# One queue or two for the loads of the first attention in a four-layer cross-attention kernel

## Chip, core and metric

The kernel runs on one core of one Trainium2 chip. The metric is the device time of one execution in microseconds (us), the median of several runs.

## What is computed

Sixteen sequences of 56 tokens with 256 channels (`x`) pass through four layers. Each of them attends to the same memory, `ctx`: 1500 keys with 128 channels for every sequence. The change concerns the first layer alone, which has a single head:

```python
memory_proj    = einsum('bme,de->bmd', memory, W_mem)              # memory: 16 x 1500 x 128
scores         = einsum('bnd,bmd->bnm', hidden_states, memory_proj) / sqrt(D)
attn           = softmax(scores, axis=-1)
memory_context = einsum('bnm,bmd->bnd', attn, memory_proj)
gate           = sigmoid(concat([hidden_states, memory_context]) @ W_gate + b_gate)
x              = rmsnorm(hidden_states + gate * memory_context)
```

Layers 2 and 4 are attention with 16 heads and a feed-forward part, layer 3 is self-attention, narrow cross-attention and a gated MLP. They take most of the time, and nothing in them is changed.

## The kernel before

**Products are reassociated.** `W_mem` is applied to the 56 queries (`pe_q0`), so the 1500 keys are used as they come from memory. That takes every batch of `ctx` in two layouts: *in channels* (`kt0`, from the input `ctxT`, 128 channels x 1500 keys, 750 KB), which the scores need, and *in keys* (`kn0`, from `ctx`, 125 partitions x 12 keys x 128 channels, 672 + 78 KB in two transfers), which the weighted sums need. Both lie in the big tile `q_and_o`, in four buffers each, one per batch: batch b is in buffer b % 4.

**Units.** Two batches make a unit u, so there are 8 units (`L0U`), and the four buffers of a layout hold two units. `pe_l0` runs ten steps s on TensorE (PE). Step s has, in this order: the scores of unit s (L639, 6 matmuls, which the trace counts as 12), the weighted sums of unit s-2 (L651, 24 matmuls, in the trace 48), and the transposes of the probabilities of unit s-1 (L665, 12). In step 0 and 1 there are no sums, in steps 8 and 9 no scores. The end of the scores of a third of the keys counts up `s_sc` (in the listings `s_scores`), so `s_sc` is 3(u+1) when the scores of unit u are complete. The end of the sums of unit u brings `s_pv` (in the listings `s_sums`) to u+1. VectorE (DVE) takes the maxima (L700) and normalises (L717); ScalarE (ACT) exponentiates (L684); both copy the transposed probabilities out of PSUM (L675, ACT two thirds, DVE one third).

**Who loads.** The channels are loaded by SyncE (SP) in `sp_l0_keysT`: batches 0 to 3 at once, and from batch 4 on unit u when the scores of unit u-2 are done (`on.wait_ge(s_sc, 3 * (u - 1))`), since these used the same buffers. The keys are loaded by ACT in `act_l0_keys`: units 0 and 1 at the start of `act_l0`, which is after the barrier that ends the query products, then unit s in step s, between the exponential of unit s and the copies of unit s-1, when the sums of unit s-2 are done (`on.wait_ge(s_pv, u - 1)`). SP and ACT each have a hardware queue of their own (q1 and q10 in the profile). A wait holds only the instruction stream of the engine that waits.

**After the last load.** SP issues the loads of the gate stage (`sp_l0_gate`, L729 to L735: `W_memT`, `W_gateT`, `b_gate`, `norm_w`, `x`, some 1.8 MB), on which `pe_l0_gate` waits, then waits at the barrier that ends the first attention, and issues the loads of the second layer (`sp_gated_a`, L817 on). The gate stage starts at L741 behind that barrier.

Of the kernel before, what the change touches and what calls it, by code (L numbers as in the profile page):

```python
# [14 lines left out]
B, S, D, C, KEYS = 16, 56, 256, 128, 1500  # L15
# [7 lines left out]
KP, KT = 125, 12  # L23
# [15 lines left out]
L0U = B // 2  # L39
# [59 lines left out]
def build(nc, io, out):  # L99
    with ExitStack() as ctx:  # L100
        def sem(name):
            return ctx.enter_context(nc.semaphore(name))
# [118 lines left out]
        kt0 = [QO_flat[:, i * KEYS:(i + 1) * KEYS] for i in range(4)]  # L221
        kn0 = [QO_flat[:, 4 * KEYS + i * KT * C:4 * KEYS + (i + 1) * KT * C] for i in range(4)]
# [58 lines left out]
        s_l0_kt = [sem(f"s_l0_keysT{i}") for i in range(4)]  # L281
        s_l0_kn = [sem(f"s_l0_keys{i}") for i in range(4)]
# [6 lines left out]
        s_sc, s_mx, s_nx = sem("s_scores"), sem("s_max"), sem("s_negmax")  # L289
        s_ex, s_rc = sem("s_exp"), sem("s_recip")  # L290
        s_tr, s_eh, s_el = sem("s_transposed"), sem("s_high"), sem("s_low")
        s_pv, s_ov = sem("s_sums"), sem("s_o_out")
# [22 lines left out]
        def join(e, on, n):  # L315

            e.drain().then_inc(s_join, 1)
            on.wait_ge(s_join, ENGINES * n)
# [296 lines left out]

        ctx_rows = io["ctx"].rearrange("b (p k) c -> b p (k c)", p=KP)

        def sp_l0_keysT(e, on):
            for b in range(B):
                if b >= 4:  # L620
                    on.wait_ge(s_sc, 3 * ((b - 4) // 2 + 1))
                e.dma_start(kt0[b % 4], io["ctxT"][b]).then_inc(s_l0_kt[b % 4], 16)

        def act_l0_keys(e, on, u):
            for b in (2 * u, 2 * u + 1):
                if u >= 2:
                    on.wait_ge(s_pv, u - 1)
                for lo, hi in ((0, 112), (112, KP)):
                    e.dma_start(kn0[b % 4][lo:hi, :], ctx_rows[b, lo:hi, :]).then_inc(s_l0_kn[b % 4], 16)

        def pe_l0(e, on):
            for s in range(L0U + 2):
# [37 lines left out]
        def l0_evacuate(e, on, u, c, done):  # L670
            on.wait_ge(s_tr, 3 * u + c + 1)
            on.wait_ge(s_pv, u - 1)
            dst = l0_p_T[u % 2][0:KP, 4 * c:4 * c + 4, 0:128]
            src = psum[3 + c][0:KP, :].rearrange("p (k r) -> p k r", k=4)
            x = e.copy(dst, src) if c < 2 else e.tensor_copy(dst, src)  # L675
            x.then_inc(done, 1)

        def act_l0(e, on):
            act_l0_keys(e, on, 0)
            act_l0_keys(e, on, 1)  # L680
            for s in range(L0U + 1):
                if s < L0U:
                    on.wait_ge(s_nx, s + 1)
                    e.activation(l0_scores[s % 2], l0_scores[s % 2], ACT.Exp, bias=mx[:, s % 2, 3:4],  # L684
                                 accum_out=mx[:, s % 2, 4:5]).then_inc(s_ex, 1)
                if 2 <= s < L0U:
                    act_l0_keys(e, on, s)
                if s:
                    for c in range(2):
                        l0_evacuate(e, on, s - 1, c, s_l0_ea)  # L690
            join(e, on, J["l0"])
# [35 lines left out]
        def sp_l0_gate(e, on):  # L727
            w = s_w["l0b"]
            e.dma_start(w_memT, io["W_memT"]).then_inc(w, 16)  # L729
            e.dma_start(w_gateT, io["W_gateT"].rearrange("(k p) n -> p k n", p=128)).then_inc(w, 16)  # L730
            e.dma_start(b_gate, io["b_gate"].to_broadcast([128, D])).then_inc(w, 16)
            e.dma_start(norm_w, io["norm_w"].to_broadcast([128, D])).then_inc(w, 16)
            e.dma_start(X, io["x"]).then_inc(w, 16)
            e.dma_start(vecs, io["vectors"]).then_inc(s_const, 16)
            e.dma_start(gates, io["gates"].to_broadcast([128, 4])).then_inc(s_const, 16)  # L735
# [79 lines left out]
        def sp_gated_a(e, on, l):  # L815
            w = s_w[f"l{l}a"]
            e.dma_start(g_wq, io[f"L{l}_Wq"].rearrange("(k p) n -> p k n", p=128)).then_inc(s_w[f"l{l}q"], 16)  # L817
            e.dma_start(g_wkT, io[f"L{l}_WkT"].rearrange("(k p) n -> p k n", p=128)).then_inc(w, 16)
            e.dma_start(value_w, io[f"L{l}_Wkv"][:, INNER:2 * INNER]).then_inc(w, 16)

        def sp_gated_b(e, on, l):
            e.dma_start(g_w1, io[f"L{l}_W1"].rearrange("(k p) n -> p k n", p=128)).then_inc(s_w[f"l{l}u"], 16)
            e.dma_start(g_w2.rearrange("p (k n) -> p k n", k=8), io[f"L{l}_W2"].rearrange("(k p) n -> p k n", p=128)).then_inc(s_w[f"l{l}d"], 16)
# [145 lines left out]
        def sp_wo(e, on, x, l):  # L969

            on.wait_ge(*x.scores((B - 1) * RT - 1, 2))
            on.wait_ge(*x.sums((B - 1) * NG - 1))
            wo = io[f"L{l}_Wo"].rearrange("(k p) n -> p k n", p=128)
            e.dma_start(wo_a.rearrange("p (k n) -> p k n", k=6), wo[:, 0:6, :]).then_inc(s_w[f"l{l}o"], 16)
            e.dma_start(wo_b.rearrange("p (k n) -> p k n", k=2), wo[:, 6:8, :]).then_inc(s_w[f"l{l}o"], 16)

        def sp_cross(e, on, x, first):
            def keysT(b):
                if b >= 2:
                    on.wait_ge(*x.scores((b - 1) * RT - 1, 2))  # L980
                e.dma_start(kt_raw[b % 2], io["ctxT"][b]).then_inc(s_ktl[b % 2], 16)

            def keys(b):
                if b >= 2:
                    on.wait_ge(*x.sums((b - 1) * NG - 1))
                for lo, hi in ((0, 112), (112, KP)):
                    e.dma_start(kn_raw[b % 2][lo:hi, :], ctx_rows[b, lo:hi, :]).then_inc(s_knl[b % 2], 16)

            def mask(b):
                if b:  # L990
                    on.wait_ge(*x.mask(b - 1))
                e.dma_start(mask_raw, io["mask"][b:b + 1, :].to_broadcast([128, KEYS])).then_inc(s_ml, 16)

            if first:
                keysT(0), keys(0), mask(0)
                keysT(1), keys(1)
            else:
                mask(1)
                for b in range(2, B):
                    mask(b), keysT(b), keys(b)  # L1000
# [359 lines left out]
        def sp_l2a(e, on):  # L1360
            on.wait_ge(*prod.made[g1.down[NT - 1]])
            w = s_w["l2a"]
            e.dma_start(wcq, io["L2_cq_w"].rearrange("(k p) n -> p k n", p=128)).then_inc(w, 16)
            e.dma_start(value_w[:, 0:2 * C], io["L2_ckv_w"]).then_inc(w, 16)
            e.dma_start(wcd, io["L2_cdense_w"]).then_inc(w, 16)
# [355 lines left out]
        def sp_narrow(e, on):  # L1721
            for b in range(B):
                if b == 1:
                    on.wait_ge(s_join, ENGINES * J["l2q"])
                if b >= 2:
                    on.wait_ge(s_n_prod, 6 * (b - 1))
                e.dma_start(KT2[b % 2], io["ctxT"][b]).then_inc(s_n_ctx[b % 2], 16)
# [320 lines left out]
        def sync(e):  # L2048
            on = Passed(e)
            w = s_w["l0"]  # L2050
            e.dma_start(w_mem, io["W_mem"].rearrange("(k p) c -> p k c", p=128)).then_inc(w, 16)
            e.dma_start(XT[:, 0:2, :], io["xT"]).then_inc(w, 16)
            e.dma_start(ident, io["ident"]).then_inc(w, 16)
            sp_l0_keysT(e, on)
            sp_l0_gate(e, on)
            on.wait_ge(s_join, ENGINES * J["l0"])
            sp_gated_a(e, on, 1)
            sp_cross(e, on, layers[0], True)
            on.wait_ge(s_join, ENGINES * J["l1q"])
            sp_cross(e, on, layers[0], False)  # L2060
            sp_wo(e, on, layers[0], 1)
            on.wait_ge(s_join, ENGINES * J["l1"])
            sp_gated_b(e, on, 1)
            sp_experts(e, on)
            sp_l2a(e, on)
            sp_narrow(e, on)
            sp_l2b(e, on)
            sp_cross(e, on, layers[1], True)
            on.wait_ge(*prod.made[gu_prod["up", 1, len(IT) - 1, 1]])
            sp_gated_a(e, on, 3)  # L2070
            sp_cross(e, on, layers[1], False)
            sp_wo(e, on, layers[1], 3)
            on.wait_ge(s_join, ENGINES * J["l3"])
            sp_gated_b(e, on, 3)
            on.wait_ge(s_join, ENGINES * J["l3ff"])
            e.dma_start(out, X).then_inc(s_out, 16)
            on.wait_ge(s_out, 16)
# [151 lines left out]
```

## Times and profile before

| | us |
|---|---|
| median of 3 runs | 2423.84 (2419.64 to 2424.02) |
| the profiled execution | 2411.01 |
| its span in the trace | 2409.2 |
| first attention in it, up to the gate stage's first matmul | 114.18 |

| engine | busy in the span |
|---|---|
| PE | 2312.6 us (96%) |
| DVE | 1577.1 us (65%) |
| ACT | 1279.2 us (53%) |
| POOL | 629.1 us (26%) |

The profile is of one execution. Shares over the whole span are means over layers with different limits. The first attention is under 5% of the span, so it has to be read by itself, in the stretch from 0 to 114 us.

### The profile page before, as it was taken

The page shows a single profiled execution, that of the slowest core. Times are in us where ns is not written, and L with a number is a line of the kernel's source. Part 1 is how long each engine was busy: PE and PEld are TensorE (multiplying, and loading weights), DVE is VectorE, ACT ScalarE, POOL GpSimd, SP SyncE. Part 2 cuts the span into 40 slices and gives each one's busy share as a digit, 9 for nine tenths or more (in the row PEclk, how much of TensorE's full clock was granted, in tenths as well). Part 3 has the DMA queues.
Part 4 walks back from the last instruction along what each step waited for, and adds up shares of the span by engine and source line. Part 5 has one row for each costly group of instructions (what it writes and reads, how often), then busy time and mean ns, then how long its engine had stood idle before and what let it go on. Part 6 is the DMA issues. An engine that isn't in the chain of part 4 may idle for free.

```text
span 2409.2 us, 41153 instructions
## 1 busy us (share of the span) xinstructions
PE 2312.6 (96%) x16032; PEld 1883.6 (78%) x16032; DVE 1577.1 (65%) x4254; ACT 1279.2 (53%) x2184; POOL 629.1 (26%) x692
## 2 busy tenths in 40 slices
PE   7978999999999999799999999899999999999999
PEld 3857999999999895456666666456799999999988
DVE  3357777777777657577777776313777777777764
ACT  1235555555555533277777777212555555555553
POOL 0024344443433315200000000010444444343330
PEclk8989999999999999899999999899999999999999
DMA  8810111121110110010000000310011212111010
GB/s 266 221 62 20 46 42 52 37 58 35 54 45 27 54 36 21 14 39 27 27 27 27 27 14 1 125 35 1 20 47 41 59 30 59 42 46 46 27 53 16
DMA packets 36131, 115.96 MB, mean 48 GB/s; under 512 B 4618, under 2 KB 18546, under 8 KB 35938
## 3 DMA queue, kind: packets, MB, share of 16 engines
q1 hardware_dynamic: 33474, 101.04, 13.8%
q10 hardware_dynamic: 2464, 12.29, 2.0%
q8 instruction: 128, 2.10, 0.4%
q14 instruction: 65, 0.53, 0.1%
HBM read 112.40 MB, written 0.92 MB: 47 GB/s over the span
## 4 chain that ended last, share of the span: by engine, by line
PE 89%; ACT 5%; DVE 4%; DMA 1%; issue 0%; ACTq 0%; SPq 0%; DVEq 0%
PE bank L1026 20%; PE bank L1013 19%; PE bank L1038 12%; PE bank L1773 7%; PE bank L555 7%; PE bank L1760 3%; PE bank L1998 3%; PE bank L1786 3%; ACT n_scores L1860 3%; PE bank L651 2%; PE bank L2010 2%; PE bank L1742 2%; PE bank L848 1%; PE bank L1746 1%; PE bank L1224 1%; PE bank L1048 1%
## 5 line engine op out<-in xcount | busy, mean ns | idle before, releaser
L1087 ACT CAST p_T_high<-bank 125x512 fp32r<-125x512 f32 x672 | 350.8, 595 | 516.8 <-PE bank L1038 516.8
L1160 DVE TENSOR_TENSOR p_T_low<-bank,p_T_high 125x512 fp32r<-125x512 f32 x672 | 422.6, 684 | 256.7 <-ACT p_T_high L1087 256.5
L1126 DVE CUSTOM_DVE_ANT_0 scores<-bank,mask 128x500 f32<-128x500 f32 x672 | 418.3, 672 | 1.6 <-PE bank L1013 1.6
L1097 ACT ACTIVATE scores<-scores,row_max 128x1500 f32<-128x1500 f32 x224 | 353.4, 1578 | 9.8 <-DVE row_max L1131 9.8
L1026 PE MATMUL bank<-p_T_high,keys_nat_high 125*128 125x256 f32 (+1 forms) x1152 | 346.0, 300 | 1.7 <-ACT inverse L1094 1.7
L1026 PE MATMUL bank<-p_T_high,keys_nat_low 125*128 125x256 f32 (+1 forms) x1152 | 346.3, 301 | 0.0
L1026 PE MATMUL bank<-p_T_low,keys_nat_high 125*128 125x256 f32 (+1 forms) x1152 | 346.2, 300 | 0.0
L1038 PE MATMUL bank<-ident,scores 128*125 128x128 f32 x2688 | 331.7, 273 | 1.5 <-ACT scores L1097 1.5
L1038 PEld LDWEIGHTS bank<-ident,scores 128*125 128x125 f32 x2688 | 319.0, 188 | 4.2 <-ACT scores L1097 4.1
L1893 DVE CUSTOM_DVE_ANT_0 n_scores<-bank,n_zeros 112x500 f32<-112x500 f32 x384 | 237.4, 674 | 91.9 <-PE bank L1760 91.9
L1013 PE MATMUL bank<-keys_T_high,q_stage_high 128*128 128x500 f32 x672 | 282.0, 420 | 11.8 <-DVE q_stage_low L1103 6.9
L1773 PEld LDWEIGHTS bank<-ident,n_scores 112*125 112x125 f32 x1536 | 187.2, 191 | 115.5 <-issue 54.9
L1013 PE MATMUL bank<-keys_T_high,q_stage_low 128*128 128x500 f32 x672 | 262.6, 391 | 0.0
L1013 PE MATMUL bank<-keys_T_low,q_stage_high 128*128 128x500 f32 x672 | 262.1, 390 | 0.0
L1773 PE MATMUL bank<-ident,n_scores 112*125 112x112 f32 x1536 | 218.3, 286 | 10.3 <-ACT q_and_o L1852 5.8
L1026 PEld LDWEIGHTS bank<-p_T_high,keys_nat_high 125*128 125x128 f32 x1152 | 216.7, 188 | 10.2 <-ACT inverse L1094 2.2
L1026 PEld LDWEIGHTS bank<-p_T_low,keys_nat_high 125*128 125x128 f32 x1152 | 217.0, 188 | 8.5
L1026 PEld LDWEIGHTS bank<-p_T_high,keys_nat_low 125*128 125x128 f32 x1152 | 216.7, 188 | 0.0
L1860 ACT ACTIVATE n_scores<-n_scores,n_stats 112x1500 f32<-112x1500 f32 x128 | 197.7, 1546 | 0.4 <-DVE n_stats L1899 0.4
L1166 POOL CAST q_stage_high<-q_and_o 128x256 fp32r<-128x256 f32 (+1 forms) x94 | 41.5, 441 | 427.6 <-PE bank L1013 427.5
L1013 PEld LDWEIGHTS bank<-keys_T_high,q_stage_high 128*128 128x128 f32 x672 | 127.7, 190 | 32.2 <-issue 8.3
L1013 PEld LDWEIGHTS bank<-keys_T_high,q_stage_low 128*128 128x128 f32 x672 | 127.1, 189 | 26.6
(237 smaller groups left out, 3492.6 us busy)
## 6 DMA issues: line engine op xcount, KB each, us to landing
ctx_T<-in_ctxT SPq DMA_DIRECT2D x32, 750.0 KB, 4.2
ctx_nat<-in_ctx SPq DMA_DIRECT2D x32, 672.0 KB
q_and_o<-in_ctxT SPq DMA_DIRECT2D x16, 750.0 KB, 9.7
n_ctx_T<-in_ctxT SPq DMA_DIRECT2D x16, 750.0 KB, 4.2
q_and_o<-in_ctx ACTq DMA_DIRECT2D x16, 672.0 KB
mask_bytes<-in_mask SPq DMA_DIRECT2D x32, 187.5 KB, 5.2
weights<-in_L_W SPq DMA_DIRECT2D x4, 1024.0 KB, 6.2
ctx_nat<-in_ctx SPq DMA_DIRECT2D x32, 78.0 KB
```

The source lines that it names most:

```text
L555: x = e.matmul(out, left[i], right[j], start=start and n == 0, stop=stop and n == 2)
L1013: m = e.matmul(psum[c][:, 0:CHK], QSs[i][g % 2][:, lo:lo + 128], KTs[j][b % 2][:, cols], start=(n == 0), stop=(n == 2))
L1026: m = e.matmul(psum[6 + g % 2][:, cols_g], KNs[i][b % 2][0:KP, cols], PTs[j][g % 2][0:KP, k, cols_g], start=(k == 0 and n == 0), stop=(k = ...
L1038: m = e.transpose(psum[3 + c][0:KP, 128 * k:128 * k + 128], SB[u % 2][:, (4 * c + k) * KP:(4 * c + k + 1) * KP], ident)
L1087: e.copy(PTs[0][g % 2][0:KP, 4 * c:4 * c + 4, lo:lo + 128], psum[3 + c][0:KP, :].rearrange("p (k r) -> p k r", k=4)).then_inc(s_eh, 1)
L1097: e.activation(SB[s % 2], SB[s % 2], ACT.Exp, bias=mx[:, s % 4, 3:4], accum_out=mx[:, s % 4, 4:5]).then_inc(s_ex, 1)
L1126: e.tensor_tensor_reduce(out=SB[u % 2][:, c * CHK:(c + 1) * CHK], in0=psum[c][:, 0:CHK], in1=mb[:, c * CHK:(c + 1) * CHK], scale=1.0, scal ...
L1160: e.tensor_tensor(low, psum[3 + c][0:KP, :].rearrange("p (k r) -> p k r", k=4), high.bitcast(F32), ALU.subtract).then_inc(s_el, 1)
L1760: e.matmul(psum[r][0:PAIR, 0:CHK], n_q[b % 2][rows, PAIR * hh:PAIR * hh + PAIR], CK[b % 2][rows, c * CHK:(c + 1) * CHK], start=True, stop= ...
L1773: m = e.transpose(psum[4 + t % 2][0:KP, PAIR * k:PAIR * k + PAIR], n_unit(quad, r)[0:PAIR, at:at + KP], ident[0:PAIR, 0:PAIR])
L1860: e.activation(unit, unit, ACT.Exp, bias=n_st[0:PAIR, quad % 2, r, 3:4], accum_out=n_st[0:PAIR, quad % 2, r, 4:5]).then_inc(s_n_ex, 1)
L1893: e.tensor_tensor_reduce(out=n_unit(quad, r)[0:PAIR, c * CHK:(c + 1) * CHK], in0=psum[r][0:PAIR, 0:CHK], in1=n_zeros[0:PAIR, :], scale=1.0 ...
```

## The change

All loads of the memory for the first attention are issued by SP, in one instruction stream and one queue. `act_l0_keys` is gone from ACT. The order in SP's stream is: channels of units 0 and 1, keys of units 0 and 1, then for u = 2 to 7 the channels of unit u and the keys of unit u, each with the wait it had before. The loads of the gate stage follow behind the keys of unit 7.

```diff
-        def sp_l0_keysT(e, on):
-            for b in range(B):
-                if b >= 4:
-                    on.wait_ge(s_sc, 3 * ((b - 4) // 2 + 1))
-                e.dma_start(kt0[b % 4], io["ctxT"][b]).then_inc(s_l0_kt[b % 4], 16)
-
-        def act_l0_keys(e, on, u):
-            for b in (2 * u, 2 * u + 1):
-                if u >= 2:
-                    on.wait_ge(s_pv, u - 1)
-                for lo, hi in ((0, 112), (112, KP)):
-                    e.dma_start(kn0[b % 4][lo:hi, :], ctx_rows[b, lo:hi, :]).then_inc(s_l0_kn[b % 4], 16)
+        def sp_l0_keys(e, on):
+            def in_channels(u):
+                for b in (2 * u, 2 * u + 1):
+                    if u >= 2:
+                        on.wait_ge(s_sc, 3 * (u - 1))
+                    e.dma_start(kt0[b % 4], io["ctxT"][b]).then_inc(s_l0_kt[b % 4], 16)
+
+            def in_keys(u):
+                for b in (2 * u, 2 * u + 1):
+                    if u >= 2:
+                        on.wait_ge(s_pv, u - 1)
+                    for lo, hi in ((0, 112), (112, KP)):
+                        e.dma_start(kn0[b % 4][lo:hi, :], ctx_rows[b, lo:hi, :]).then_inc(s_l0_kn[b % 4], 16)
+
+            in_channels(0), in_channels(1)
+            in_keys(0), in_keys(1)
+            for u in range(2, L0U):
+                in_channels(u)
+                in_keys(u)
...
         def act_l0(e, on):
-            act_l0_keys(e, on, 0)
-            act_l0_keys(e, on, 1)
             for s in range(L0U + 1):
                 if s < L0U:
                     on.wait_ge(s_nx, s + 1)
                     e.activation(l0_scores[s % 2], l0_scores[s % 2], ACT.Exp, bias=mx[:, s % 2, 3:4],
                                  accum_out=mx[:, s % 2, 4:5]).then_inc(s_ex, 1)
-                if 2 <= s < L0U:
-                    act_l0_keys(e, on, s)
                 if s:
                     for c in range(2):
                         l0_evacuate(e, on, s - 1, c, s_l0_ea)
...
-            sp_l0_keysT(e, on)
+            sp_l0_keys(e, on)
```

SP's stream in the first attention before. After the four channels without a wait come those of units 2 and 3 (the pattern goes on to unit 7), in pairs:

```order
L622 DMA q_and_o<-in_ctxT 128x1500 x4
L622 DMA q_and_o<-in_ctxT 128x1500 [waits s_scores]
L622 DMA q_and_o<-in_ctxT 128x1500
L622 DMA q_and_o<-in_ctxT 128x1500 [waits s_scores]
L622 DMA q_and_o<-in_ctxT 128x1500
```

The same stream now, from the channels of unit 2 to those of unit 3:

```order
L623 DMA q_and_o<-in_ctxT 128x1500 [waits s_scores]
L623 DMA q_and_o<-in_ctxT 128x1500
L630 DMA q_and_o<-in_ctx 112x1536 [waits s_sums]
L630 DMA q_and_o<-in_ctx 13x1536
L630 DMA q_and_o<-in_ctx 112x1536
L630 DMA q_and_o<-in_ctx 13x1536
L623 DMA q_and_o<-in_ctxT 128x1500 [waits s_scores]
L623 DMA q_and_o<-in_ctxT 128x1500
```

Between the two pairs of channels there are now four transfers of keys, the first of which waits for `s_sums`, that is, for the weighted sums of unit 0.

PE's stream in step 3 is the same before and now. The scores of unit 3 (first and second row: the channels of its two batches), the sums of unit 1, and the start of the transposes of unit 2:

```order
L639 MATMUL bank0<-q_and_o 64x500 [waits s_max,s_l0_keysT2]
L639 MATMUL bank0<-q_and_o 64x500 [waits s_l0_keysT3]
L639 MATMUL bank1<-q_and_o 64x500 [waits s_max]
L639 MATMUL bank1<-q_and_o 64x500
L639 MATMUL bank2<-q_and_o 64x500 [waits s_max]
L639 MATMUL bank2<-q_and_o 64x500
L651 MATMUL bank7<-area,q_and_o 128x64 [waits s_l0_keys2,s_l0_evac_dve,s_l0_evac_act]
L651 MATMUL bank7<-area,q_and_o 128x64 x11
L651 MATMUL bank7<-area,q_and_o 128x64 [waits s_l0_keys3]
L651 MATMUL bank7<-area,q_and_o 128x64 x11
L665 MATMUL bank3<-ident,area 125x128 [waits s_l0_normed]
```

Nothing moved here: the sums of a unit stand behind the scores of the unit that comes two later.

ACT's stream before, from the exponential of unit 2 to that of unit 3:

```order
L684 ACTIVATE area,row_max<-area,row_max 128x1500 [waits s_negmax]
L629 DMA q_and_o<-in_ctx 112x1536 [waits s_sums]
L629 DMA q_and_o<-in_ctx 13x1536
L629 DMA q_and_o<-in_ctx 112x1536
L629 DMA q_and_o<-in_ctx 13x1536
L675 COPY area<-bank3 125x4x128 [waits s_transposed]
L675 COPY area<-bank4 125x4x128 [waits s_transposed]
```

and now, where the copies follow the exponential directly (the rows of units 2 and 3):

```order
L689 ACTIVATE area,row_max<-area,row_max 128x1500 [waits s_negmax]
L682 COPY area<-bank3 125x4x128 [waits s_transposed]
L682 COPY area<-bank4 125x4x128 [waits s_transposed]
L689 ACTIVATE area,row_max<-area,row_max 128x1500 [waits s_negmax]
L682 COPY area<-bank3 125x4x128 [waits s_sums,s_transposed]
```

## Rows read from the trace of the kernel before

**Rows 1.** The page: busy time of each engine, then the chain by engine.
```profile
PE 2312.6 (96%) x16032; PEld 1883.6 (78%) x16032; DVE 1577.1 (65%) x4254; ACT 1279.2 (53%) x2184; POOL 629.1 (26%) x692
...
PE 89%; ACT 5%; DVE 4%; DMA 1%; issue 0%; ACTq 0%; SPq 0%; DVEq 0%
```

**Rows 2.** Chain that ended last, first attention: start us, us, what.
```profile
14.76 4.32 PE bank L639 x12
19.46 14.90 DMA q_and_o<-in_ctxT
34.41 5.26 PE bank L639 x10
39.67 5.52 PE bank L651 x48
45.19 1.36 PE bank L665 x12
46.55 2.67 PE bank L639 x12
49.22 5.50 PE bank L651 x48
...
87.34 5.52 PE bank L651 x48
94.28 0.42 ACTq L629
94.75 1.08 ACT area L675 x2
95.87 8.86 PE bank L651 x48
104.73 2.66 PE bank L665 x12
...
114.18 3.29 PE bank L741 x14
```

**Rows 3.** Waits: line waited for: us in total, times, longest us.
```profile
PE bank L639 <- DMA q_and_o<-in_ctxT: 8.0, 2, 6.0
PE bank L651 <- ACT area L675: 1.7, 1, 1.7
...
SPq L622 <- PE bank L639: 59.5, 6, 17.1
```

**Rows 4.** Timeline: start us, us, engine, line, count, in brackets the idle before.
```profile
2.20 66.93 SPq L622 DMA_DIRECT2D q_and_o<-in_ctxT  x16
14.78 3.99 ACTq L629 DMA_DIRECT2D q_and_o<-in_ctx  x8
30.49 1.93 PE L639 MATMUL bank<-q_and_o 128*64 128x500 f32 x2 [5.99 <-DMA q_and_o<-in_ctxT]
94.25 0.69 DVE L675 COPY area<-bank 125x512 f32<-125x512 f32 x1
```

**Rows 5.** Stretches: from:to, busy us, last the granted clock, DMA share, GB/s.
```profile
2.00:13.90 11.90, 6.10 (x8) 2.52 (x8) 0.62 (x1) 1.07 (x1) 0.97 (x1) 1.00 0.96 349
19.10:34.40 15.30, 6.11 (x26) 2.25 (x22) 5.71 (x15) 4.23 (x6) 0.00 (x0) 0.83 1.01 273
34.41:39.67 5.26, 5.26 (x11) 1.30 (x11) 1.37 (x4) 0.00 (x0) 0.00 (x0) 0.50 0.49 202
39.67:45.20 5.53, 5.53 (x50) 5.53 (x51) 0.84 (x3) 1.64 (x2) 0.00 (x0) 1.00 0.78 280
94.20:97.90 3.70, 2.04 (x18) 2.03 (x18) 0.74 (x2) 1.07 (x2) 0.00 (x0) 0.97 1.04 237
98.00:107.40 9.40, 9.39 (x44) 9.10 (x43) 0.28 (x1) 1.17 (x2) 0.00 (x0) 0.50 0.49 126
116.00:124.00 8.00, 7.28 (x28) 4.99 (x27) 2.33 (x6) 3.79 (x6) 4.51 (x4) 1.00 1.04 383
124.00:128.00 4.00, 4.00 (x21) 3.51 (x20) 0.66 (x2) 0.50 (x2) 3.92 (x4) 1.00 1.03 263
```

## Prediction

> **What bounds the kernel now.** I read the page first. PE is busy for 96% of the span and makes up 89% of the chain [rows 1]. That is a mean over four layers, and the change touches only the first 114 us, so the next view is the chain of waits there [rows 2]. The reader is to see two regimes. Once it runs, the chain is PE alone: sums 5.50 us, transposes 1.36, scores 2.67, and again. From 49.22 to 87.34 us that is four steps, 9.53 us each. Loads don't show in it, because the channels of unit u+1 are asked for a whole step before PE wants them. At 19.46 the chain shows the other regime: 14.90 us of a transfer in channels, then ten score matmuls in 5.26 us. There PE outran the loads.
>
> The waits say the same [rows 3]. PE waited for channels twice, 8.0 us in total, and for a copy by ACT once, 1.7 us. SP spent 59.5 us in six waits for the scores: it is early, and sits ready when a buffer comes free. That readiness is what the change touches.
>
> The last view is the stretches with clock and bandwidth [rows 5]. The ten score matmuls after the wait ran at a granted clock of 0.50, that is 1.2 of 2.4 GHz, 0.53 us each against 2.67/12 = 0.22 us at 1.00. PE had idled 5.99 us before the first pair of them [rows 4]. So a wait of PE for a load costs the wait and a slow start.
>
> **The change, part by part.** Let T(s) be the end of the sums in step s. Before, T(2) is 45.19 and T(7) is 87.34 + 5.52 = 92.86 [rows 2].
>
> *The wait in front of the channels.* SP now meets the keys of unit u, which wait for `s_pv` = u-1, before it may issue the channels of unit u+1. That count comes at T(u), from the sums in step u. PE wants the channels of unit u+1 as soon as it has done the transposes, 1.36 us after T(u). Before, they were issued at the end of the scores in step u-1, a step and a half earlier. Now six issues stand between T(u) and the scores, and the keys lie ahead of the channels in the same queue: two keys, then two channels, 4 x 768 KB = 3.07 MB. This comes five times, for the scores of units 3 to 7.
>
> How long? For the channels the nearest row is the pair issued at 39.67: in 5.53 us 280 GB/s moved 1.55 MB, which is the pair (1.536 MB), with the DMA engines busy for 0.78 of it, 4.3 us. So 1.2 us pass before data flow, and the pair takes 4.3 [rows 5]. For the keys the row nearest to one layout alone is 124 to 128 us, the second layer's keys and mask from SP's queue, at 263 GB/s: 1.536/0.263 = 5.8 us. Sum 1.2 + 5.8 + 4.3 = 11.3 us from T(u) to the second batch of channels. Bounds: all at the best stretch, 383 GB/s, 1.2 + 8.0 = 9.2 us; all at the worst full one, 237 GB/s, 1.2 + 13.0 = 14.2 us [rows 5].
>
> The 16 DMA engines top out at 435 GB/s by the Trainium skill (DMA: Bandwidth & Descriptors, Specifications); by that figure, as an estimate, the two pairs take 8.3 us with the start, and the sum below comes out 15 us lower. No stretch here reaches it: the best is 383 [rows 5].
>
> *The slow start.* When the second batch lands, one score matmul pair is done and ten remain, as at 34.41: 5.26 us at half clock. The idle before the first batch is longer here (about 7.7 us) than the 5.99 there [rows 4]. The sums behind them then run at full clock, 5.52, as from 39.67 [rows 5]. Step: 11.3 + 5.3 + 5.5 = 22.1 us instead of 9.53. Five steps: 110.5 instead of 47.7 us.
>
> *The start.* The first keys are issued behind the first channels at about 4 us, not at 14.78 after the barrier [rows 4]. They can't move sooner than the channels are through, at about 13.9 (from 2 to then 349 GB/s moved the 4.2 MB issued first) [rows 5]. Keys of four batches and channels of unit 2 are 4.6 MB; at the 273 GB/s that this mix had from 19.1 to 34.4 [rows 5] they land by 13.9 + 16.9 = 30.8 instead of 34.4. T(2) becomes 30.8 + 5.3 + 5.5 = 41.6, a gain of 3.6 us. Then T(7) = 41.6 + 110.5 = 152.1 instead of 92.86.
>
> *ACT without the issues.* In steps 3 to 7 ACT's four issues (1.6 us) lay beside the sums and scores, so taking them out is worth nothing there. At the end they show: ACT copied at 94.75 behind its last issue, at 94.28, and PE waited until 95.87 [rows 2]. DVE's copy, from 94.25 for 0.69 us [rows 4], ends at 94.94, so the gain is 0.9 us. From 98 to 107.4 the clock then stood at 0.50 [rows 5]: sums in 8.86 instead of 5.52, transposes in 2.66 instead of 1.36 [rows 2], 4.6 us. With half the pause I take it that the clock stays up; the other end of the range has it fall as before. From T(7) to the gate stage: 21.3 before, now 21.3 - 0.9 - 4.6 = 15.8 us.
>
> *The loads behind.* The keys of unit 7 and the gate stage's 1.8 MB are issued from T(7) on, not at 69 us. 1.2 + 3.36/0.263 = 14.0 us is less than 15.8, so I cost them at nothing; the cover is the last two sums. At 225 GB/s they would end 0.3 us late, and the end of the range allows 2 us. The 32 issues that SP takes over (about 0.4 us each) fall in its waits.
>
> *Sum.* Gate stage at 152.1 + 15.8 = 167.9 instead of 114.18: **+53.7 us**. Nothing behind it moves: the second layer's loads hang on the same barrier. On the profiled execution's 2411.01 that gives 2464.7. This execution is 12.8 us under the median of the runs, so I add the difference to the median: 2423.84 + 53.7 = 2477.5 us.
>
> **The rivals.**
> - *The clock stays up in the stalls.* For it: PE is busy for half of each step. Against: the 0.50 after 5.99 us of idling. Ten score matmuls take 2.2 us, a step 19.0, the five 95.0: +38.2, 2462 us. Chance 0.12.
> - *The clock stays down through the sums as well*, as from 98 to 107.4 [rows 5]. Then scores cost 5.3, sums 8.9, a step 25.5, T(7) = 45.0 + 127.5 = 172.5, the end 20.4: +78.7, 2503 us. Against: after 34.41 it rose within 5.3 us. Chance 0.05.
> - *Only issue time moves.* All of SP's 32 new issues fit into its 59.5 us of waits [rows 3], the bytes are the same, so nothing is gained or lost: 2424 us. It decides if SP's stall on `s_sums` costs PE nothing, for which the channels would have to land within 1.4 us of T(u). They need 9.2 at the least. Chance 0.03. It is the rule of the Trainium skill (Trainium Kernel Development and Optimization, Key Constraints): transfers of all queues share the 16 DMA engines, and issuing from several engines "only saves the sequencer's issue time". It leaves out the waits that a stream holds.
> - *Faster.* The first keys flow without a gap, ACT copies at once, and the clock stays up at the end: -3.6 - 0.9 - 4.6 = -9.1, 2415 us. For it: each of the three stands in the rows. It decides if the five stalls cost less than 9.1/5 = 1.8 us each; I have 12.6. Chance 0.03.
>
> **How the numbers follow.** The forecast has a chance of 0.77. Its own range has a step of 20.0 to 25.0 us (load 9.2 to 14.2), which gives +43.2 to +68.2, and with a fallen clock and late loads at the end up to +74.8. The first rival is taken in, the second left out. Range: 2458 to 2499 us. A measurement of this kernel can tell about 0.2%, 4.8 us. Faster by more: 0.03, within: 0.03, slower: 0.94, from the same cases.
>
> **What would show it.** In the changed profile: PE waits for channels in six steps instead of one, some 49 us in total (8.9 in each of five, and 4.4 left of the 8.0); SP's longest waits are for the sums (L651 of before), not for the scores; steps of about 22 us, with a granted clock of 0.50 in the scores and 1.00 in the sums; DMA idle in the second half of each step; the gate stage's first matmul at about 168 us, and the same time as before from there on. It is wrong if the steps stay near 9.5 us, if the keys and channels of a step take clearly under 9.2 us, or if the gate stage waits for its own loads.

## Result, and the profile after

| | before | changed |
|---|---|---|
| median of 4 runs, us | 2422.53 (2419.64 to 2424.02) | 2469.91 (2467.43 to 2473.90) |
| profiled execution, us | 2411.01 | 2470.97 |
| its span, us | 2409.2 | 2469.2 |
| gate stage's first matmul, us | 114.18 | 168.27 |

The changed kernel is slower by the factor 1.0203, interval 1.0189 to 1.0217, which is 46 to 53 us; the medians differ by 47.4 us. 53.7 was forecast, just above that interval.

The page of the changed kernel, busy time and queues:

```profile
PE 2330.4 (94%) x16032; PEld 1887.3 (76%) x16032; DVE 1576.5 (64%) x4254; ACT 1278.1 (52%) x2184; POOL 628.9 (25%) x692
...
q1 hardware_dynamic: 35938, 113.33, 15.3%
```

The work is the same; PE's share fell from 96% [rows 1] to 94%, and q10, ACT's queue, is gone. The chain of waits in the first attention of the changed kernel (start us, us, what):

```profile
29.48 6.72 PE bank L646 x12
36.20 5.51 PE bank L658 x48
41.73 0.33 SPq L630
...
43.38 9.12 DMA q_and_o<-in_ctxT
52.54 5.44 PE bank L646 x12
57.98 5.51 PE bank L658 x48
63.51 0.33 SPq L630
...
65.16 9.17 DMA q_and_o<-in_ctxT
74.38 6.46 PE bank L646 x12
...
146.88 5.50 PE bank L658 x48
152.38 0.50 PE bank L672 x4
...
154.58 5.54 PE bank L658 x48
...
162.31 5.56 PE bank L658 x48
```

Where before the chain was PE alone [rows 2], each step now goes from the sums (L658) to SP's issues of the keys (L630), from there to a transfer of channels, and only then back to the scores. T(u), the end of the sums in step u, is 41.71, 63.49, 86.35, 108.10, 130.74 and 152.38 us: steps of 21.6 to 22.9 us, 22.1 in the mean. The waits, of PE and of SP (line waited for: us in total, times, longest us):

```profile
PE bank L646 <- DMA q_and_o<-in_ctxT: 52.6, 6, 9.7
...
SPq L630 <- PE bank L658: 119.6, 6, 22.0
SPq L623 <- PE bank L646: 11.0, 1, 11.0
```

PE waits for channels in six steps. SP waits before the keys for the sums, and never again for the scores after unit 2. Before, SP stood ready and PE waited 8.0 us [rows 3]. When the second batch of channels was there shows in the row of the weight loads (PEld) for the second pair of score matmuls; in this first step of the five it is 54.38 - 41.71 = 12.7 us after T(2), where PE had begun the first pair at + 10.8:

```profile
54.38 0.30 PEld L646 LDWEIGHTS bank<-q_and_o 128*64 128x64 f32 x4 [1.54 <-DMA q_and_o<-in_ctxT]
```

The stretches of one step in the changed kernel (last the granted clock, DMA share, GB/s): the transfers, the last ten score matmuls, the sums; then the end.

```profile
42.90:52.40 9.50, 0.17 (x2) 0.00 (x0) 0.89 (x2) 0.40 (x1) 0.00 (x0) 0.66 0.99 280
...
54.50:58.00 3.50, 3.50 (x11) 0.96 (x11) 1.37 (x4) 0.00 (x0) 0.00 (x0) 0.76 0.00 0
58.00:63.50 5.50, 5.50 (x50) 5.50 (x51) 0.84 (x3) 1.64 (x2) 0.00 (x0) 1.00 0.00 0
154.00:166.00 12.00, 10.59 (x93) 10.46 (x94) 1.44 (x3) 1.07 (x2) 0.00 (x0) 1.00 0.98 272
```

PE and the DMA engines now take turns: engines full and PE idle for 9.5 us, then no transfer at all during the last ten score matmuls and the sums. In the kernel before both ran at once, with the clock at 1.00, from 46.5 to 92.8 us:

```profile
46.50:92.80 46.30, 46.30 (x350) 36.35 (x350) 19.94 (x53) 13.56 (x20) 0.00 (x0) 1.00 1.02 287
```

In the changed kernel, at the end the clock stays at 1.00, and the gate stage's loads, at 272 GB/s, are hidden behind the last two sums.

**Behind the first attention.** The second layer's first load is 54.1 us later than before, the third layer's 55.9 us, and the MLP's 61.1 us. The last 5.1 us come between the first load of the narrow attention and the first of the MLP, where no instruction differs; the experiments say what they are.

### The profile page after: what moved, and what is told of

It is laid out like the page before. It is cut to its first block, busy times and chain, and to the rows that moved or that the text cites. A ratio compares the mean times of both kernels' runs of the same rounds, so it can differ in the third digit from the quotient of the medians.

```text
span 2469.2 us, 41160 instructions
## 1 busy us (share of the span) xinstructions
PE 2330.4 (94%) x16032; PEld 1887.3 (76%) x16032; DVE 1576.5 (64%) x4254; ACT 1278.1 (52%) x2184; POOL 628.9 (25%) x692
## 4 chain that ended last, share of the span: by engine, by line
PE 87%; ACT 5%; DVE 4%; DMA 3%; issue 1%; POOL 0%; SPq 0%; ACTq 0%; DVEq 0%; POOLq 0%
PE bank L1029 19%; PE bank L1016 18%; PE bank L1041 12%; PE bank L1776 7%; PE bank L555 6%; PE bank L1763 3%; PE bank L2001 3%; PE bank L1789 3%; ACT n_scores L1863 2%; DMA q_and_o<-in_ctxT 2%; PE bank L658 2%; PE bank L2013 2%; PE bank L1745 2%; PE bank L646 2%; PE bank L851 1%; PE bank L1749 1%
```

## The experiments

In each trace T(2), T(7) and the start of the gate stage are read from the timeline of PE (ends of the sums of steps 2 and 7). Ratios are against runs of the kernel before on the same chip.

| run | T(2) | T(7) | gate stage | median, us | ratio (interval) |
|---|---|---|---|---|---|
| before | 45.2 | 92.9 | 114.2 | | |
| changed | 41.7 | 152.4 | 168.3 | 2469.9 | 1.0203 (1.0189 to 1.0217) |
| e1 before again | 43.2 | 91.3 | 112.1 | 2420.6 | 0.9990 (0.9974 to 1.0007) |
| e2 order of release | 42.1 | 89.7 | 105.7 | 2410.3 | 0.9938 (0.9923 to 0.9953) |
| e3 wait alone | 46.0 | 168.1 | 194.1 | 2490.3 | 1.0272 (1.0234 to 1.0311) |
| e4 channels first | 41.1 | 122.8 | 138.8 | 2441.9 | 1.0073 (1.0048 to 1.0097) |
| e5 copies first | 45.9 | 93.5 | 117.8 | 2418.3 | 0.9994 (0.9979 to 1.0009) |
| e6 first keys by SP | 41.1 | 88.7 | 115.6 | 2420.3 | 0.9986 (0.9968 to 1.0004) |
| e7 both, two queues | 40.4 | 88.2 | 117.8 | 2416.2 | 0.9979 (0.9967 to 0.9992) |
| e8 alternating | 40.7 | 158.7 | 183.4 | 2485.3 | 1.0265 (1.0243 to 1.0288) |
| e9 gate loads late | 43.6 | 92.6 | 113.6 | 2418.1 | 0.9988 (0.9975 to 1.0001) |
| e10 changed again | 40.6 | 150.6 | 166.6 | 2468.2 | 1.0198 (1.0175 to 1.0222) |
| e11 before, third | 43.7 | 91.9 | 119.0 | 2419.5 (one run) | |
| e12 before, fourth | 43.1 | 90.7 | 118.2 | 2424.8 (one run) | |

### The kernel before, again

No edit.

> The kernel before, unchanged, with a second profile. The first attention should last the same again (gate stage's first matmul at 114.2 us, within 0.5). The question is the rest: between the narrow layer's first load and the MLP's first load the changed kernel's trace is 5.1 us longer than that of before, though no instruction there is changed. If that is variation between executions, this profile may be some us longer there as well; if it comes from the change, this profile shows 905.3 and 1518.7 us again (613.3 us between them), within 1 us.

The narrow layer took 621.9 us (903.85 to 1525.75) in this trace, against 613.3 in the first. So its length varies between executions without any edit. Over all fourteen traces it is 613.3 to 622.0 us. The 5.1 us in the changed kernel's trace are within such variation. The first trace of before has the shortest of the fourteen, which is a part of why it lies some 12 us under the median of its kernel.

### One queue, in the order in which buffers come free

```diff
             in_keys(0), in_keys(1)
+            in_channels(2), in_channels(3)
             for u in range(2, L0U):
-                in_channels(u)
+                if u + 2 < L0U:
+                    in_channels(u + 2)
                 in_keys(u)
```

> One queue, every load issued by SP, but in the order in which the buffers come free: channels of unit u+2 ahead of keys of unit u. Theory 1 (SP's stream holds the channels behind a wait for the sums): all five stalls go, steps of 9.5 us, T(2) at 41.7 as in the changed kernel, T(7) at 89.4, the end as in the changed kernel (15.9 us), gate stage at 105.3 us: 62.9 us earlier than the changed kernel and 8.9 earlier than the kernel before, so about 2413 us. Theory 2 (a single queue itself is too slow for both layouts, or SP can't issue them in time): steps well above 9.5 us, the gate stage at 130 us or later.

Timeline of PE in this run (start us, us, line, count, in brackets the idle before):

```profile
30.04 6.58 PE L648 MATMUL bank<-q_and_o 128*64 128x500 f32 x12 [5.92 <-DMA q_and_o<-in_ctxT]
36.55 5.57 PE L660 MATMUL bank<-area,q_and_o 125*128 125x64 f32 x48
...
43.42 2.74 PE L648 MATMUL bank<-q_and_o 128*64 128x500 f32 x12
46.08 5.57 PE L660 MATMUL bank<-area,q_and_o 125*128 125x64 f32 x48
...
105.67 3.29 PE L746 MATMUL bank<-weights,q_and_o 128*128 128x256 f32 x14 [0.42 <-DVEq L317]
```

All five stalls are gone, the steps are 9.53 us, with every load still in SP's one queue. Theory 1 stands. The cost of the change is the order of the waits in SP's stream, not the number of queues. With the order repaired, this version beats the changed kernel by some 2.5% and the kernel before by 0.6%. Its gate stage starts 10.1 us before the mean of the four traces of before (115.8 us, below); the medians differ by 13.7, and the rest was not traced.

### The wait without the queue

```diff
                 if b >= 4:
                     on.wait_ge(s_sc, 3 * ((b - 4) // 2 + 1))
+                if b >= 6:
+                    on.wait_ge(s_pv, b // 2 - 2)
```

> Two queues as before, the keys issued by ACT, but the channels of unit u+1 (from unit 3 on) also wait for the sums of step u. This is the wait of the changed kernel without the keys ahead of the channels in the same queue. Theory 1a (both pairs share the DMA engines, whatever the queue): channels land about 10 us after T(u), a little sooner than the 10.8 of the changed kernel, steps of 20 to 21.5 us, gate stage at 160 to 167 us. Theory 1b (the place behind the keys is what costs): channels land 5.5 to 6 us after T(u), steps of 14 to 17 us, gate stage at 135 to 150 us.

Chain of this run, then its stretch of the transfers after T(2):

```profile
46.11 0.33 SPq L624
...
46.48 12.80 DMA q_and_o<-in_ctxT
...
59.33 5.00 PE bank L641 x10
```

```profile
47.30:59.20 11.90, 2.01 (x3) 0.29 (x2) 0.81 (x2) 1.07 (x2) 0.00 (x0) 0.63 0.88 251
```

Both of my figures were too low, and I had compared with the wrong one: 10.8 us is the first batch of the changed kernel, its second comes at 12.3 to 12.9. Here the second channels are there 13.2 us after T(2) and 13.1 to 15.4 after the other four, and the steps are 24.4 us in the mean, worse than in the changed kernel. So the wait by itself is enough for the whole loss, and a second queue does not soften it: the keys, issued at the same moment by ACT, travel at the same time. By how much it is worse is less sure, since there are only two runs, 2480.8 and 2499.9 us, and the trace is of the longer. Behind T(7) the clock had fallen as well (26 us to the gate stage instead of 16).

### The channels ahead of the keys

```diff
+            in_channels(2)
             for u in range(2, L0U):
-                in_channels(u)
+                on.wait_ge(s_pv, u - 1)
+                if u + 1 < L0U:
+                    in_channels(u + 1)
                 in_keys(u)
```

> One queue, the wait for the sums in front of the channels of unit u+1 stays, but the keys of unit u come behind them. Theory 1: the channels have the engines to themselves and land 5.5 us after T(u) (1.2 + 4.3); PE idles some 2 us before the first batch and 2 more before the second. With the clock at full speed a step is 5.5 + 2.3 + 5.5 = 13.3 us, with it fallen 5.5 + 5.3 + 5.5 = 16.3; I expect 13.3 to 14.5, since the idle is short. Gate stage at 41.7 + 5 x 13.3 + 16 = 124 to 140 us. If the order in the queue does not decide (engines take both at once), steps stay near 21 us.

Timeline of PE in step 3, then the stretches of channels and of keys behind them:

```profile
45.55 1.93 PE L649 MATMUL bank<-q_and_o 128*64 128x500 f32 x2 [3.04 <-DMA q_and_o<-in_ctxT]
48.19 4.43 PE L649 MATMUL bank<-q_and_o 128*64 128x500 f32 x10 [0.70 <-DMA q_and_o<-in_ctxT]
52.55 5.57 PE L661 MATMUL bank<-area,q_and_o 125*128 125x64 f32 x48
```

```profile
42.30:46.50 4.20, 1.16 (x4) 0.31 (x3) 0.94 (x2) 0.45 (x1) 0.00 (x0) 0.80 0.91 355
46.50:52.00 5.50, 4.79 (x11) 1.18 (x10) 0.86 (x3) 0.00 (x0) 0.00 (x0) 0.53 1.02 259
```

The first batch lands 4.0 to 4.4 us after T(u), the second at 6.4 to 7.0, 6.6 in the mean, against 12.7 in the changed kernel. Steps average 16.3 us, so the place behind the keys costs 22.1 - 16.3 = 5.8 us a step, and the wait for the sums the remaining 16.3 - 9.5 = 6.8. That is the forecast's sum split in two: its price for two batches of keys was 5.8 us, and the second channels come 6.1 us sooner without them. Its 5.5 us for the channels alone was 1.1 too low. The slow start came even with an idle of 3.04 us: the clock is 0.53 in the second stretch. I had expected it to stay up, and steps of 13.3 to 14.5 us. The keys move at 259 GB/s, the channels at 355.

### The gains of the change, one by one

ACT's copies ahead of its loads:

```diff
-                if 2 <= s < L0U:
-                    act_l0_keys(e, on, s)
                 if s:
                     for c in range(2):
                         l0_evacuate(e, on, s - 1, c, s_l0_ea)
+                if 2 <= s < L0U:
+                    act_l0_keys(e, on, s)
```

> The kernel before, with ACT's copies ahead of its key loads in each step: the part of the change that frees ACT's stream, by itself. Theory: the wait of PE for ACT at the end (1.66 us before) shrinks to 0.8, and the clock stays up over the last sums and transposes, so T(7) to the gate stage is 15.8 us instead of 21.3, and the gate stage starts at 108.7 us. Rival: unit 7's keys, issued some 2 us later and sharing the engines with the gate stage's loads, come late; then the pause only moves to the last sums (PE waits for keys, 1 to 3 us), the clock may fall all the same, and the stage starts at 111 to 115 us.

The first keys by SP:

```diff
-            sp_l0_keysT(e, on)
+            sp_l0_keysT(e, on, 0, 4)
+            act_l0_keys(e, on, 0)
+            act_l0_keys(e, on, 1)
+            sp_l0_keysT(e, on, 4, B)
```

with the same two lines taken out of `act_l0`, and `sp_l0_keysT` taking the first and the last batch as arguments.

> The kernel before, with only the keys of units 0 and 1 issued by SP behind the first channels; all later keys by ACT as before. It isolates the start. Theory: channels of unit 2 land at 29.5 to 31 instead of 34.4, T(2) is 41.7 instead of 45.2, the steps stay at 9.5, the gate stage starts 3.5 us earlier, at 110.7. Rival: the two queues then fall behind in steps 3 to 7, since DMA is busy throughout there, and the gain is given back: gate stage at 113 to 115.

Both edits together:

> Both of the above in one: first keys by SP, ACT's copies ahead of its loads, still two queues. Against the run with one queue in the order of release (gate stage at 105.7, ratio 0.9938). Theory N (the number of queues is neutral): gate stage at 105 to 106.5, ratio 0.993 to 0.995. Theory M (transfers of two queues in flight at once move fewer bytes per us: 3.07 MB took 13.2 us with two queues after a common wait, and 10.8 in one queue): a wait for channels or for unit 7's keys shows, gate stage at 107 to 112.

Timelines of PE behind T(7), first with the copies ahead, then with the first keys by SP, then with both:

```profile
96.68 9.13 PE L651 MATMUL bank<-area,q_and_o 125*128 125x64 f32 x48 [1.76 <-DMA q_and_o<-in_ctx]
...
109.30 8.09 PE L651 MATMUL bank<-area,q_and_o 125*128 125x64 f32 x48 [0.83 <-issue]
```

```profile
91.81 2.86 PE L651 MATMUL bank<-area,q_and_o 125*128 125x64 f32 x24 [1.64 <-DMA q_and_o<-in_ctx]
95.81 5.38 PE L651 MATMUL bank<-area,q_and_o 125*128 125x64 f32 x24 [1.14 <-DMA q_and_o<-in_ctx]
```

```profile
92.97 10.39 PE L651 MATMUL bank<-area,q_and_o 125*128 125x64 f32 x48 [3.37 <-DMA q_and_o<-in_ctx]
103.16 2.87 PE L665 MATMUL bank<-ident,area 128*125 128x128 f32 x12
106.86 10.47 PE L651 MATMUL bank<-area,q_and_o 125*128 125x64 f32 x48 [0.83 <-issue]
```

The rival's wait for keys showed each time, but the gate stage lies above the range that each expectation gave for it (117.8, 115.6 and 117.8 us), and with the first keys by SP steps 3 to 7 kept their 9.5 us, so the queues did not fall behind there. T(2) and T(7) come 4 to 5 us sooner than in the first trace of before when SP issues the first keys (2.7 to 3.5 against the mean of its four). Then PE waits for the keys of unit 6, and the sums behind it take 8 to 10.5 us instead of 5.5, at the lower clock. The pause only changed its cause. From T(7) to the gate stage these take 24.3, 26.8 and 29.6 us, against 15.9 in the changed kernel and in the one-queue version of e2. Each is one execution, and the kernel before itself takes 20.8 to 27.4 us there in its four traces, so the first two lengths are within what it does by itself; and the trace of both edits together is of the slowest of their twelve runs, 2422.8 us. Alone, neither edit can be told from no change; together they give 0.2% by the runs.

### Alternating between the layouts

After the wait for the sums, one queue carries keys, channels, keys, channels, a batch each:

```diff
+            in_channels(2)
             for u in range(2, L0U):
-                in_channels(u)
-                in_keys(u)
+                on.wait_ge(s_pv, u - 1)
+                for b in (2 * u, 2 * u + 1):
+                    for lo, hi in ((0, 112), (112, KP)):
+                        e.dma_start(kn0[b % 4][lo:hi, :], ctx_rows[b, lo:hi, :]).then_inc(s_l0_kn[b % 4], 16)
+                    if u + 1 < L0U:
+                        e.dma_start(kt0[(b + 2) % 4], io["ctxT"][b + 2]).then_inc(s_l0_kt[(b + 2) % 4], 16)
```

> The changed kernel with its wait for the sums, one queue, but the four batches that follow T(u) alternate: keys, channels, keys, channels. It asks whether the slower transfers of the two-queue run come from alternating between the layouts. If alternating by whole batches costs nothing, the second channels land 10.8 us after T(u) as in the changed kernel, the first ones some 4 us sooner, and the step is 21.5 to 22 us, gate stage at 165 to 168. If alternating costs as much as two queues did, they land 13 us after T(u) and the gate stage starts at 176 to 180.

```profile
48.46 1.93 PE L651 MATMUL bank<-q_and_o 128*64 128x500 f32 x2 [6.37 <-DMA q_and_o<-in_ctxT]
53.63 4.78 PE L651 MATMUL bank<-q_and_o 128*64 128x500 f32 x10 [3.25 <-DMA q_and_o<-in_ctxT]
```

The first channels come at T(2) + 7.8 us and serve nothing, because PE can do only one pair with them; the second come at + 12.9, after which the ten score matmuls take 4.8 us. The expectation's 10.8 us for the second batch of the changed kernel was that of its first; the second comes at + 12.7 there, too. So alternating delays it by some 0.2 us (12.1 to 13.1 in the five steps, 12.8 in the mean), and the engines move about as much: 257 GB/s from 41.9 to 53.6 us here, 263 in the changed kernel from 42.9 to 54.4. A step is still longer, 23.6 us against 22.1. What differs is what PE does before the ten: in the changed kernel it comes to them straight from the first pair and needs 3.3 to 4.6 us (3.9 in the mean), here it has idled 2.9 to 3.7 us since that pair and needs 4.8 to 5.3 (5.1). Grouping is thus worth about 1.2 us a step in the clock; that the idle time is the reason is read from these rows and was not tested by itself. By T(7) that makes 6.3 us; the rest of the difference, up to 183.4 us, is the clock, which had fallen behind T(7) here (24.7 us to the gate stage).

### The gate stage's loads held back

The two-queue version of e7 with one wait more:

```diff
             sp_l0_keysT(e, on, 4, B)
+            on.wait_ge(s_pv, L0U - 2)
             sp_l0_gate(e, on)
```

> The two-queue version with first keys by SP and ACT's copies ahead of its loads, and now SP also holds the gate stage's loads back until the sums of step 7 are done, as one queue does by its order. Theory G (the gate stage's loads, issued at 64 us, take bandwidth from the keys of units 6 and 7): PE's wait of 3.4 us for keys is gone, the clock stays up, the gate stage starts at 105 to 107 us, ratio about 0.994. Theory M (two queues mixing the layouts are slower by themselves): some wait for keys or a fallen clock remains, gate stage at 109 or later.

```profile
84.37 2.73 PE L639 MATMUL bank<-q_and_o 128*64 128x500 f32 x10 [0.23 <-DMA q_and_o<-in_ctxT]
...
94.79 5.54 PE L651 MATMUL bank<-area,q_and_o 125*128 125x64 f32 x48 [0.83 <-ACT area L675]
...
102.53 2.86 PE L651 MATMUL bank<-area,q_and_o 125*128 125x64 f32 x24 [0.83 <-ACT area L675]
107.83 5.38 PE L651 MATMUL bank<-area,q_and_o 125*128 125x64 f32 x24 [2.44 <-DMA q_and_o<-in_ctx]
```

The wait of 3.37 us before the sums of unit 6 is gone, so by this trace the gate stage's loads had caused it. But it comes back one step later: the gate stage's loads and unit 7's keys now leave within 1 us of each other in two queues, and the second batch of keys is 2.44 us late. In one queue the keys are ahead, and no wait shows. In this stage a single queue is therefore a gain: its order decides who waits. The theory that only the early start of the loads mattered falls half; the trace does not settle whether two queues also move fewer bytes by themselves. T(2) is 43.6 us here, with the first keys by SP as in the two runs before, which had 41.1 and 40.4: the gain at the start is not there in every execution.

### Both kernels once more

> The changed kernel again, with a second profile. Gate stage's first matmul at 167 to 169 us, as in the first. The narrow layer, from its first load to the MLP's first load, took 618.5 us in the first profile and 613.3, 621.9, 622.0 and 614.7 in four kernels that don't differ there: this one should lie anywhere between 613 and 622. The median over the runs should be 47 to 54 us above that of the kernel before.

> A third profile of the kernel before. Against the timed medians the changed kernel is 48 to 49 us slower and the one-queue version in order of release 15 us faster, but against the two traces of before their first attention differs by +54 and -7.5 us: both are off by 6 to 7 us the same way. If the first attention of before often ends later than in its two profiles (unit 7's keys late, clock fallen, as in three two-queue variants, 24 to 30 us from T(7) to the gate stage instead of 21), then one of two further profiles should show a gate stage at 116 us or later. If both show 112 to 115, the difference lies elsewhere and stays open.

> A fourth profile of the kernel before, the same question as the third: gate stage at 116 us or later in at least one of the two, or 112 to 115 in both.

The changed kernel's second trace repeats the first: gate stage at 166.6 us, narrow layer 617.4 us, 48 us above before. The third and fourth of the kernel before don't repeat theirs. Here the third, behind T(7), the timeline of PE and the stretch:

```profile
94.99 9.58 PE L651 MATMUL bank<-area,q_and_o 125*128 125x64 f32 x48 [1.67 <-ACT area L675]
104.36 2.87 PE L665 MATMUL bank<-ident,area 128*125 128x128 f32 x12
108.06 10.48 PE L651 MATMUL bank<-area,q_and_o 125*128 125x64 f32 x48 [0.83 <-issue]
118.95 5.44 PE L741 MATMUL bank<-weights,q_and_o 128*128 128x256 f32 x14 [0.41 <-DVEq L317]
```

```profile
94.00:118.00 24.00, 22.18 (x107) 21.91 (x107) 1.01 (x3) 2.10 (x4) 0.00 (x0) 0.54 0.33 79
```

After the same pause as in [rows 2] the clock stays at 0.5 up to the gate stage, which starts at 119.0 and 118.2 us. Over four traces of the kernel before the gate stage starts at 115.8 us in the mean, over two of the changed kernel at 167.4: +51.6 us. So a part of the distance between the +54.1 of the first pair of traces and the 47 to 49 us of the runs is that the first trace of before ended its first attention 1.6 us before that mean, and the first of the changed kernel 0.9 us behind its own.

## Why the prediction was right

The median is 2469.91 us, forecast 2477.5, inside the range of 2458 to 2499. The mechanism is the one forecast: a wait in front of the channels and a slow start behind it, five times. That the step came out at 22.1 us to the tenth is luck, because two of its terms were off by 1.4 us each, in opposite directions. By its own steps:

- **The wait in front of the channels.** Forecast: 1.2 + 5.8 + 4.3 = 11.3 us to the second batch. Measured: 12.3 to 12.9, 12.7 in the mean of the ten steps of two traces, so 1.4 too short. The keys cost 6.1 us (e4 against the changed kernel) instead of 5.8, the channels 6.6 (e4) instead of 5.5. The row behind the 5.5 counted bytes: nearly all of that pair had moved by 45.2 us, but its second batch, issued at 40.07, took 6.8 us to land, 7.1 from the first issue at 39.70. PE waited 52.6 us in six steps, forecast 49. The order of release (e2) takes the five stalls away, the wait alone (e3) brings them back with two queues, and the channels ahead of the keys (e4) removes 5.8 us a step. All of the loss is in this wait and the slow start that it brings.
- **The slow start.** Forecast 5.3 us for the ten matmuls behind the second batch, as after the wait before; measured 3.3 to 4.6, 3.9 in the mean, so 1.4 too long. The row taken had PE idle for 1.98 us between the first pair and the ten; here the first pair runs straight into them. The clock is 0.50 in the first pair, 0.76 over the ten in the step shown, and 1.00 in the sums. The rival with the clock up is out, and the one with the clock down through the sums too, in the changed kernel.
- **The start.** T(2) forecast 41.6, measured 41.7 and 40.6. With the first keys alone moved (e6) it is 41.1. The gain of 3.6 us was taken against a T(2) of 45.2, the latest of the four traces of before (43.1 to 45.2); against their mean it is 2.6.
- **The end.** 15.8 us from T(7) forecast, 15.9 and 16.0 measured, the clock up in both traces. That half the pause leaves the clock up was taken without a row for it; it held in four traces (both of the changed kernel, e2, e4), and in e8 the clock fell behind the same 0.83 us. The loads behind were hidden as said: `x_nat` landed 9.3 us after its issue at 157.2, 1.7 us ahead of the gate stage.
- **The sum.** 167.9 us for the gate stage, 168.3 measured. The other side of it was off: I took the kernel before from one trace, in which T(7) to the gate stage is 21.3 us. In its second it is 20.8, in its third and fourth 27.1 and 27.4, since the clock stayed down for longer. By the mean of all traces the loss is 51.6 us. What is then left to the medians, about 3 us, is less than what the narrow layer alone varies by; it was not traced further.
- **The rival by the Trainium skill** (Trainium Kernel Development and Optimization, Key Constraints: issuing from several engines "only saves the sequencer's issue time"). With the order of release it holds as far as bandwidth goes: one queue for both layouts lost nothing (e2). Read as a forecast for this change it failed by 47 us, because a second stream is also a second place to wait: in the changed kernel SP's waits for the sums (119.6 us in six) held back the channels behind them.
- **The faster rival** named three gains. e2 has them together, without the stalls, and is 0.6% faster; taken singly in two queues (e5, e6) they can't be told from no change.

## What to carry to other kernels

Loads that wait for buffers can share one stream only if they stand in the order in which the buffers come free. Write down for each load when its wait is met and when its data are wanted; a load behind a wait that is met later inherits that wait. A single queue is also a tool: what is wanted first goes ahead, which two queues did not do here (e7, e9). Take the landing of a load from the row that waits for it, and not from the bytes moved. Take the kernel before from more than one trace, where its clock or its lengths vary.

## What was not expected of the hardware

- The order of four equal transfers in one queue hardly decides when the last of them is there: keys, keys, channels, channels at + 12.3 to 12.9 us, alternating + 12.1 to 13.1 (e8). In two queues at once it is + 13.1 to 15.4, in one trace (e3).
- The granted clock fell to 0.53 in the scores after an idle of only 3.04 us (e4). Behind pauses of 1.66 us it fell for 9 us in one trace of the kernel before and for over 20 us in two others, with PE busy nearly all the time; in the remaining one (e1) the sums behind the same pause ran at full speed, and only those behind a second pause of 1.63 us did not:

```profile
94.41 5.57 PE L651 MATMUL bank<-area,q_and_o 125*128 125x64 f32 x48 [1.66 <-ACT area L675]
...
102.97 8.71 PE L651 MATMUL bank<-area,q_and_o 125*128 125x64 f32 x48 [1.63 <-DMA q_and_o<-in_ctx]
```

- Behind two pauses of 0.83 us the last sums ran at full speed (5.5 us) in e2, e4 and both traces of the changed kernel, but not in e8 (8.0 and 10.5 us).
- The keys (112 + 13 partitions) moved at 259 GB/s where the channels (128 partitions) moved at 355 (e4), from the same queue.
